# A linear recurrence run by halves of its tokens, with row 1's gate products placed between the halves of row 0's output projection

## The reference, cut to what matters

```
h   = rmsnorm(x) * ln1_w
x_in = h @ w_in.T                                  # 256 channels: two chunks of 128
gate = sigmoid(h @ w_gate.T)
a    = sigmoid(a_param + x_in @ w_a.T)
state[t] = a[t] * state[t-1] + sqrt(1 - a[t]^2 + 1e-8) * x_in[t]      # over 1024 tokens
y    = gate * state
x    = x + y @ w_out.T
h2   = rmsnorm(x) * ln2_w
x    = x + (silu(h2 @ w_mlp_gate.T) * (h2 @ w_mlp_up.T)) @ w_mlp_down.T
```

## Time and profile before

| | us |
|---|---|
| median of three runs | 669.39 |
| lowest and highest | 668.39, 670.0 |
| the profiled execution | 667.37 |
| its span in the trace | 665.6 |
| PE busy of the span | 604.7 (91%) |
| DVE busy | 518.3 (78%) |
| ACT busy | 377.8 (57%) |
| POOL busy | 112.7 (17%) |

### The profile page before, as it was taken

The page is one execution under the profiler, slowest core; times in us unless marked ns, Lnnn a source line. Parts: engine busy times, 40 slices in busy tenths (PEclk is TensorE's granted clock), DMA queues, the critical chain, the costliest instruction groups (busy, mean ns, idle before and its releaser), DMA issues.

```text
span 665.6 us, 9214 instructions
## 1 busy us (share of the span) xinstructions
PE 604.7 (91%) x3304; PEld 239.3 (36%) x3304; DVE 518.3 (78%) x927; ACT 377.8 (57%) x692; POOL 112.7 (17%) x140
## 2 busy tenths in 40 slices
PE   7968899999999698899999998999999988998997
PEld 5434445545456262222222122222222222334443
DVE  5556867854869987997997988999999996339634
ACT  3845122422500206786887777888888889962231
POOL 5932021100104551103012000000100012011000
PEclk9979999999999989999999999999999999998999
DMA  7100000000131211201201001010010000000001
GB/s 233 53 1 0 1 0 1 0 1 0 43 115 50 95 66 31 91 2 51 70 12 48 2 30 29 2 43 13 21 38 2 1 1 1 1 1 0 12 21 32
DMA packets 18989, 20.22 MB, mean 30 GB/s; under 512 B 3968, under 2 KB 12672, under 8 KB 18944
## 3 DMA queue, kind: packets, MB, share of 16 engines
q1 hardware_dynamic: 16900, 18.55, 8.8%
q0 software_dynamic: 656, 0.59, 0.3%
q10 hardware_dynamic: 1388, 0.50, 0.3%
HBM read 15.23 MB, written 4.19 MB: 29 GB/s over the span
## 4 chain that ended last, share of the span: by engine, by line
PE 63%; DVE 22%; ACT 6%; DMA 2%; issue 2%; DVEq 2%; ACTq 1%; POOLq 0%; POOL 0%
PE banks L1595 17%; PE banks L1581 13%; DVE negmax L1161 9%; PE banks L1508 7%; PE banks L1297 7%; PE banks L1379 5%; PE banks L1422 3%; ACT arena L855 3%; PE banks L1370 2%; PE banks L1310 2%; DVE arena L1015 2%; DVE arena L1068 1%; PE banks L1523 1%; ACT arena L845 1%; DMA bo<-in_bo 1%
## 5 line engine op out<-in xcount | busy, mean ns | idle before, releaser
L1161 DVE TENSOR_REDUCE negmax<-banks 128x2 f32<-128x1024 f32 x256 | 301.5, 1221 | 23.9 <-PE banks L1508 20.6
L855 ACT ACTIVATE arena<-banks 128x512 f32<-128x512 f32 x512 | 267.9, 606 | 84.8 <-PE banks L1581 83.9
L1581 PE MATMUL banks<-arena 59*128 59x512 bf16 x512 | 148.5, 382 | 7.1 <-ACT arena L855 5.7
L1508 PE MATMUL banks<-arena 56*128 56x512 bf16 x512 | 120.4, 385 | 22.4 <-DVE negmax L1161 21.1
L1595 PE MATMUL banks<-arena 128*32 128x512 f32 x1024 | 136.4, 605 | 0.6 <-ACT arena L855 0.6
L1581 PEld LDWEIGHTS banks<-arena 59*128 59x128 bf16 x512 | 37.8, 94 | 150.5 <-ACT arena L855 135.1
L1379 PE MATMUL banks<-arena,bT 128*128 128x512 f32 x128 | 60.1, 593 | 1.6 <-ACT arena L693 1.6
L571 POOL TENSOR_TENSOR rstd<-veps,neghalf 128x4 f32<-128x4 f32 (+1 forms) x24 | 27.1, 1130 | 200.9 <-DVE veps L929 153.7
L693 ACT ACTIVATE arena<-banks 128x512 f32<-128x512 f32 (+1 forms) x56 | 32.3, 597 | 49.4 <-PE banks L1297 20.7
L1508 PEld LDWEIGHTS banks<-arena 56*128 56x128 bf16 x512 | 26.0, 93 | 71.0 <-DVE negmax L1161 65.3
L1015 DVE TENSOR_SCALAR arena<-banks,bi 128x512 f32<-128x512 f32 x32 | 23.9, 746 | 33.0 <-PE banks L1379 33.0
(11 more groups left out here) (148 smaller groups left out, 659.8 us busy)
## 6 DMA issues: line engine op xcount, KB each, us to landing
arena<-qk_scratch SPq DMA_DIRECT2D x124, 48.0 KB
arena<-in_tab SPq DMA_DIRECT2D x4, 1024.0 KB, 6.2
qk_scratch<-arena SPq DMA_DIRECT2D x8, 384.0 KB, 2.6
out<-x SPq DMA_DIRECT2D x4, 256.0 KB, 2.3
arena<-qk_scratch SPq DMA_DIRECT2D x62, 16.0 KB
x<-in_x POOLq DMA_DIRECT2D x1, 512.0 KB, 8.2
arena<-nm_part SPq DMA_DIRECT2D x32, 4.0 KB, 1.7
x<-in_x SPq DMA_DIRECT2D x1, 256.0 KB, 3.4
```

The source lines that it names most:

```text
L855: act.activation(probs[s % 2][:, h, :], score_bank(g, n), ACT.Exp, scale=SCALE).then_inc(exp_done, 1)
L1161: return dve.tensor_reduce(negmax[:, buf, keys, :, at_tile], slot, axis=AXX, op=ALU.max, negate=True)
L1508: last = pe.matmul(slot[:, side, :], qs[rows, buf, pair, t * P:(t + 1) * P], ks[rows, buf, pair, keys * HALF:(keys + 1) * HALF], start=Tru ...
L1581: pe.matmul(score_bank(g, n), ks[rows, g % BUFS, pair, t * P:(t + 1) * P], qs[rows, g % BUFS, pair, q * HALF:(q + 1) * HALF], start=True, ...
```

## The change

`roots` works by halves: four instructions of 512 columns a row, both chunks of the first half first. `scan(b, h)` takes a half of the tokens and runs both chunks; the second half's scan starts from the last state of the first half, which is read from memory. The gate product is written over the gate and no longer over the states, since the last state is still needed, and WO reads it there. `y_ready` counts half chunks, and each half of WO waits for its own two. In the plan `rec_out` and `gate` are for one half, and the flip back is a stage of its own, `rec_back`. Row 0's stages now run WO.0.0, G.1.0, flip of WO.0.0, WO.0.1, G.1.1, flip of WO.0.1. WO.1.0 stands between up(0) and up(1), and the filler stands ahead of WO.1.1. On DVE the calls keep their places: scan(1, 0), now both chunks of the first half, before products(0), and scan(1, 1) between products(0) and products(1).

```diff
-MIXER_PLAN = (("rec_in", 0), ("rec", 0), ("gate", 0), ("rec_in", 1), ("rec", 1), ("rec_out", 0), ("gate", 1), ("turn", 0), ("up", 0), ("up", 1), ("rec_out", 1), ("down", 0),
+MIXER_PLAN = (("rec_in", 0), ("rec", 0), ("gate", (0, 0)), ("gate", (0, 1)), ("rec_in", 1), ("rec", 1),
+              ("rec_out", (0, 0)), ("gate", (1, 0)), ("rec_back", (0, 0)), ("rec_out", (0, 1)), ("gate", (1, 1)), ("rec_back", (0, 1)),
+              ("turn", 0), ("up", 0), ("rec_out", (1, 0)), ("up", 1), ("rec_out", (1, 1)), ("rec_back", (1, 0)), ("rec_back", (1, 1)), ("down", 0),
...
     if stage == "rec_out":
-        return [(f"WO.{n}.{h}", "act") for h in range(2)] + [(f"Rrec.{n}.{h}", "dve") for h in range(2)]
+        return [(f"WO.{n[0]}.{n[1]}", "act")]
+    if stage == "rec_back":
+        return [(f"Rrec.{n[0]}.{n[1]}", "dve")]
...
                 sT = rec[b][3]
-                for c in range(REC):
-                    act.wait_ge(one_minus_sq, REC * b + c + 1)
-                    act.activation(sT[:, c, :], sT[:, c, :], ACT.Sqrt, bias=tiny[:]).then_inc(root_ready, 1)
+                for h in range(2):
+                    for c in range(REC):
+                        act.wait_ge(one_minus_sq, REC * b + c + 1)
+                        act.activation(half(sT[:, c, :], h), half(sT[:, c, :], h), ACT.Sqrt, bias=tiny[:]).then_inc(root_ready, 1)
...
-            def scan(b, c):
+            def scan(b, h):
 
                 xinT, gT, aT, sT, yT = rec[b]
-                dve.wait_ge(root_ready, REC * b + c + 1)
-                dve.tensor_tensor(sT[:, c, :], sT[:, c, :], xinT[:, c, :], ALU.mult)
-                dve.drain()
-                dve.tensor_tensor_scan(yT[:, c, :], aT[:, c, :], sT[:, c, :], 0.0, ALU.mult, ALU.add)
-                dve.drain()
-                dve.wait_ge(*emptied(f"G.{b}.1.{c}"))
-                dve.tensor_tensor(yT[:, c, :], yT[:, c, :], gT[:, c, :], ALU.mult).then_inc(y_ready, 1)
+                at_ = slice(h * HALF, (h + 1) * HALF)
+                for c in range(REC):
+                    dve.wait_ge(root_ready, 2 * REC * b + REC * h + c + 1)
+                    dve.tensor_tensor(sT[:, c, at_], sT[:, c, at_], xinT[:, c, at_], ALU.mult)
+                    dve.drain()
+                    dve.tensor_tensor_scan(yT[:, c, at_], aT[:, c, at_], sT[:, c, at_], yT[:, c, HALF - 1:HALF] if h else 0.0, ALU.mult, ALU.add)
+                    dve.drain()
+                    dve.wait_ge(*emptied(f"G.{b}.{h}.{c}"))
+                    dve.tensor_tensor(gT[:, c, at_], yT[:, c, at_], gT[:, c, at_], ALU.mult).then_inc(y_ready, 1)
...
             one_minus(0)
-            for c in range(REC):
-                scan(0, c)
+            for h in range(2):
+                scan(0, h)
             add_rec(0)
...
                 elif stage == "rec_out":
-                    if n:
-                        keep_busy(f"WO.{n}.0", BUSY_SCAN)
-                    pe.wait_ge(y_ready, REC * (n + 1))
-                    for h in range(2):
-                        dense(f"WO.{n}.{h}", [(w_outT[:, k, :], half(rec[n][4][:, k, :], h)) for k in range(REC)])
-                    for h in range(2):
-                        back("WO", "Rrec", n, h)
+                    b, h = n
+                    if n == (1, 1):
+                        keep_busy(f"WO.{b}.{h}", BUSY_SCAN)
+                    pe.wait_ge(y_ready, REC * (2 * b + h + 1))
+                    dense(f"WO.{b}.{h}", [(w_outT[:, k, :], half(rec[b][1][:, k, :], h)) for k in range(REC)])
+                elif stage == "rec_back":
+                    back("WO", "Rrec", *n)
```

More of the change, by code:

```diff
@@ L135, in stage_jobs @@
     if stage == "gate":
-        return [(f"G.{n}.{h}.{c}", "act") for h in range(2) for c in range(REC)]
+        return [(f"G.{n[0]}.{n[1]}.{c}", "act") for c in range(REC)]
     if stage == "rec_out":
-        return [(f"WO.{n}.{h}", "act") for h in range(2)] + [(f"Rrec.{n}.{h}", "dve") for h in range(2)]
+        return [(f"WO.{n[0]}.{n[1]}", "act")]
+    if stage == "rec_back":
+        return [(f"Rrec.{n[0]}.{n[1]}", "dve")]
     if stage == "turn":
@@ L797, in recurrent, with recurrent_gate @@
                         act.activation(rec[b][3][:, c, :], aT[:, c, :], ACT.Square).then_inc(squared, 1)
-            def recurrent_gate(b):
-                for h in range(2):
-                    for c in range(REC):
-                        take(f"G.{b}.{h}.{c}", half(rec[b][1][:, c, :], h), ACT.Sigmoid)
+            def recurrent_gate(b, h):
+                for c in range(REC):
+                    take(f"G.{b}.{h}.{c}", half(rec[b][1][:, c, :], h), ACT.Sigmoid)
             def gates(q):
@@ L819, in _ @@
                 elif stage == "gate":
-                    recurrent_gate(n)
+                    recurrent_gate(*n)
                 elif stage == "rec_out":
-                    for h in range(2):
-                        take(f"WO.{n}.{h}", half(oT[:, n], h))
+                    b, h = n
+                    take(f"WO.{b}.{h}", half(oT[:, b], h))
                 elif stage == "turn":
@@ L1456, in recurrent, with recurrent_gate @@
                         dense(f"A.{b}.{h}.{c}", [(chunk(w_joint, c), half(hT[:, b], h))])
[L1458 to L1461, removed]
+            def recurrent_gate(b, h):
+                for c in range(REC):
+                    dense(f"G.{b}.{h}.{c}", [(chunk(w_gateT, c), half(hT[:, b], h))])
             for stage, n in MIXER_PLAN:
```

## The result

The changed kernel takes 662.78 us in the median of six runs (661.99 to 665.23), beside 668.5 for six runs of the kernel before. The ratio is 0.9927, with an interval of 0.991 to 0.9943: 3.8 to 6.0 us faster, 4.9 in the middle (the two medians lie 5.7 apart; the ratio is used from here on). The forecast was 664.3 and 5.1. The profiled execution of the changed kernel was the longest of the six: 665.23 us, with a span of 663.4. Its trace shows the clock low in stages that the change doesn't touch as well, and for that reason stages are compared by the distance between two marks in one trace and not by spans.

The account below looks back on a forecast made before the run. Bound by hand-overs between DVE, PE and ACT from 26 to 90 us, dearer by a fallen clock. Gains of 5.9 us less 0.8 for the clock gave 5.1: 664.3 us from 669.39, range 662.3 to 667.0.

Parts of the forecast that it names:

- The hand-over in row 0: Row 0, DVE to PE: the 6.62 us stall goes, the second half's add starts at 43.0, 4.7 us gained.
- the half chunk: DVE's product, scan and gate product over half the tokens: 2.67 us each, a row's four 10.7 us.
- Row 1: Row 1's stretch: halves cost 1.05 us, WO.1.0 off the path saves 1.7, the half root 0.5.
- The sum without the clock: 26 to 90 us: 0.5 + 4.2 + 0.5 − 1.05 + 1.7 = 5.9 us gained, 5.1 to 6.5 with unknown terms.
- The clock: PE's three gaps: a fall on the path costs 1.6 us; the third weighed at one half, 0.8 us off.
- Falls at both the first and the third gap: Rival, PE: two clock falls on the path leave 2.7 us gained, 666.7 us; chance 0.15.
- No fall: Rival: the clock never falls in PE's gaps, so the whole 5.9 us is gained, 663.5 us; chance 0.26.
- Dear halves: Rival, DVE's second-half scans starting from memory: 1 us more each leaves 1.9 gained, 667.5 us; chance 0.06.
- The rival of no effect: Row 0: PE starts WO.0.1 cold and late, Rrec.0.1 comes no earlier than 47.67; 669.2 us; chance 0.04.
- The slower rival: PE stays at 1.2 GHz from the first gap until MD is through: 15 us more, 678 us; chance 0.04.
- no stall of DVE above 2 us between 28 and 75: Sign of being right: DVE's timeline from 28 to 75 us shows no wait above 2 us.
- the second add, put no later than 43.5: Sign of being wrong, row 0 on DVE: the second half's add comes later than 43.5.

Follow-up runs that it names:

- 14 fillers: Changed kernel with 14 instead of 7 fillers before the first flip of Tmlp.0; ratio to the kernel before 0.9928.
- the warm projection: Kernel before with 22 fillers on PE between row 1's A products and the wait for row 0's scans; ratio 0.9976, 1.6 us faster.
- the cut alone: Roots and scans by halves in both rows, but PE waits for a whole row and keeps the plan of before; ratio 1.0048, 3.2 us slower.

## Why the prediction was right, point by point

**The hand-over in row 0** held. The output projection of the first half runs under the scans of the second, DVE's first add needs no wait, and what is late next is Rrec.0.1 behind G.1.1, as named: a wait of 1.73 us where 1.5 was put. Measured from row 1's A products, the second add came 47.67 − 29.24 = 18.43 us later before and 43.15 − 28.70 = 14.45 now: 3.98 gained, where the sum had 4.67. What was mis-sized is mainly the half chunk. Row 0's four took 11.09 us (27.75 to 38.84) and not 10.7. Scans that start from memory take 1.28 us, in row 1 against 1.22 for those that start from zero, so the start costs at most the 0.06 between them, within its bounds; but row 0's first product took 0.83 and three of its four scans 1.28 to 1.32, one of the first half among them; why, no run tells. The other 0.2 is the path from the last half chunk through WO.0.1 to the add, 4.31 us instead of 4.1, and the first half root, 0.73 us on the chain and not 0.63.

**Row 1** held nearly to the tenth. Without the clock, row 1's first product would be 4.44 us earlier (2.77 in the trace and the 1.67 of the fall): the 3.98, and 0.46 for the half root, put at 0.5. The first two half chunks took 5.34 us, as predicted, the second two 5.46, the eight products 5.57. Filler, four records and flips took 71.49 to 77.55, with the 1.72 us of WO.1.0 saved. WO.1.0 itself was covered, and so was up(1). The sum without the clock is 3.98 + 0.46 − 1.20 + 1.72 = 4.96 us by the trace, where 5.9 was put, with a lower bound of 5.1 that it just misses: the difference is row 0's 0.7, and some 0.2 of row 1's halves (1.20 where 1.05 was put) and of the roots.

**The clock** was the right term with the right price and the wrong place. Three gaps of 1.96, 2.09 and 2.12 us came where 1.8, 1.8 and 2.3 were forecast. A fall behind the first cost 1.67 and one behind the third 1.6, where 1.6 was put for each. The first was given no weight in the sum and the third one half; in the profiled execution it was the first that fell, and over all the profiles the third fell in one of eight and the first in two of three. That the forecast of 5.1 meets the 4.9 so well is therefore partly luck: a sum 0.9 too high met a clock term of 0.8, of which the median of the executions shows little (14 fillers, which remove the fall, leave the ratio where it was). The forecast time was 1.5 us too high, and 0.9 of that is the kernel before, whose median was 669.39 in three runs and 668.5 in six.

**The rivals.** Falls at both the first and the third gap were seen in no profile. No fall, 663.5, is nearer than the forecast to four of the six executions; but their sum was smaller than 5.9, and no trace of theirs tells whether the clock fell. The Trainium skill (TensorE: Matmul & The Clock Gate, HAM oscillation) ties lost clock to longer gaps than these. The traces don't agree: gaps of 1.96 and 2.12 us lost it here, in some executions. Dear halves had a small part: at most 0.06 us for each start from memory, not 1. The rival of no effect fell: the second add came 3.98 us earlier. The slower rival fell: the low stretch lasted from 46 to 50 and TensorE came back while it worked.

**The signs.** One sign of being right could not hold: no stall of DVE above 2 us between 28 and 75. The stall before row 1's first product belongs to norm, flips and square root, which the prediction itself kept in its path; it is 3.79 us without the fall and 5.42 with it. MD comes 3.29 us earlier against the A products and would come 4.96 earlier without the fall, where 5.9 was put. One sign of being wrong was just touched: the second add, put no later than 43.5, came at 43.15 on its own trace, but 14.45 us behind the A products, which is 43.69 on the time axis of the kernel before. Held were the clock of 1.00 from 33 to 44, WO.0.0 at 33.52 and up(1) done in time.

**What the prediction passed over**: the fillers. It counted those before WO.1.1 as 3.0 us of the path and asked only what the change takes off. That they need not be there at all, since the wait that they once stood in is gone, was worth 1.2 us to the changed kernel and 2.3 to the one before. With the 1.6 us of the warm projection that makes 3.9 us that the kernel before seems to hold without any halves (some 5.1 by the distances), against the 4.9 (4.96) of the change. This is a sum of two runs and not shown: no run has both edits on the kernel before.

## What to carry to other kernels

A serial recurrence can be cut where one stage waits for all of it: the cut makes the pieces together dearer than the whole (here by 1.2 to 1.3 us of VectorE a row, of which the half root wins back 0.4), and paid here only together with waits by halves and an order of stages that uses them, since with the cut alone the kernel was slower. When a stall goes, look at what the engine's own order puts in front of the next hand-over, and at filler written for the wait that has gone: moving one stage of two matmuls and dropping 23 fillers was worth 3.9 us here, where the change itself was worth 4.9. Before work is cut into pieces, see what the fillers of the order at hand cost. Compare such a stage by two marks within one trace: six executions of the changed kernel lay 3.2 us apart, and in the two profiles followed above the stages that nobody touched moved the lead of the changed kernel from 3.8 us to 1.5 and back to 2.8.

## What the runs showed of the hardware that was not expected

The same gap of 2.1 us in front of the same 26 filler records lost the clock in one execution (0.50 from 70 to 73, 4.79 us) and not in another (3.17 us), a difference of 1.6 us between two executions of one kernel. Between 33 us and MD the thirteen profiles hold 24 gaps of 1.96 to 2.21 us, and 9 of them lost the clock; the longer ones, of 5.76 to 6.68 us, all did, and no gap below 1.9 us did. The nine are not spread evenly: of the gaps behind up(0) all five lost it where up(1) follows, as in the order of before, and one of eight where WO.1.0 follows; why, no run tells.

The 26 records took 3.0 us each time, and leaving them out was worth more than a fall costs: 2.25 us of distance in the changed kernel and some 2.8 in the one before, against 1.6 to 1.7. In the four profiles without them the clock stayed at 1.00 from WO.1.1 (in the kernel before, all of WO.1) through MD, behind gaps of 0.52, 1.57, 2.21 and 2.21 us.
